# One-core transformer kernel: the feed-forward pipeline re-ordered and its residual added by TensorE, 71 expert tiles, an early square-root table, constants on GpSimd

## What is computed

```
x = x + 0.5 * ffn4(layernorm(x))     phase 0: FP4 feed-forward, hidden width 352
x = x + attn0(layernorm(x))          phase 1: low-rank causal attention
x = x + 0.5 * ffn4(layernorm(x))     phase 2
x = x + 0.5 * moe(layernorm(x))      phase 3: 8 experts, top 2, hidden width 512
x = x + attn1(layernorm(x))          phase 4: windowed attention
x = x + 0.5 * moe(layernorm(x))      phase 5

ffn4(x): g = q(x) @ q(w_gate).T;  u = q(x) @ q(w_up).T
         y = q(silu(g) * u) @ q(w_down).T
q(v):    per block of 16: scale = max|v| / 6, v / scale rounded to {0, .5, 1, 1.5, 2, 3, 4, 6}, times scale
moe(x):  each token goes to its 2 best experts:
         sum of weight * ((silu(x @ wg) * (x @ wu)) @ wd)
```

## Time and profile before

| what | value |
|---|---|
| median of three runs | 1475.54 us (1475.27 to 1479.11) |
| the profiled execution, its own time | 1479.2 us |
| its span, first to last instruction | 1477.4 us |
| mean granted TensorE clock | 0.895 |
| busy: TensorE, VectorE, ScalarE, GpSimd | 1116.1, 957.7, 823.1, 641.8 us |
| chain that ended last, by engine | TensorE 50%, VectorE 26%, DMA 6%, issue 6%, ScalarE 5% |

### The profile page before, as it was taken

One profiled execution on the slowest core, in us unless ns is written; L12 is line 12 of the kernel. 1 busy time (PEld: TensorE's weight loads), 2 busy tenths in 40 slices (PEclk: granted clock), 3 DMA queues, 4 the chain that ended last, 5 costly groups with the idle time before them and its releaser, 6 DMA issues.

```text
span 1477.4 us, 33914 instructions
## 1 busy us (share of the span) xinstructions
PE 1116.1 (76%) x11222; PEld 861.8 (58%) x11223; DVE 957.7 (65%) x1786; ACT 823.1 (56%) x1419; POOL 641.8 (43%) x924
## 2 busy tenths in 40 slices
PE   0577548999984776369999915998998636999991
PEld 0355425666653544259999902555554315999991
DVE  5799848888846997853333365889998385333333
ACT  0444236777654443246666662667766524666666
POOL 2122254344301222036766713666776302776671
PEclk9999959999997999669999956999999856999996
DMA  8100024333300000201111133353344020111115
GB/s 254 30 1 0 1 44 67 53 59 65 52 17 1 0 0 0 58 20 48 49 46 46 48 123 58 64 81 63 58 83 63 2 57 17 50 47 47 45 49 182
DMA packets 161060, 75.54 MB, mean 51 GB/s; under 512 B 125643, under 2 KB 153044, under 8 KB 160980
## 3 DMA queue, kind: packets, MB, share of 16 engines
q1 hardware_dynamic: 151508, 55.06, 17.6%
q0 software_dynamic: 9472, 19.42, 4.4%
HBM read 28.69 MB, written 15.86 MB: 30 GB/s over the span
## 4 chain that ended last, share of the span: by engine, by line
PE 50%; DVE 26%; DMA 6%; issue 6%; ACT 5%; SPq 4%; POOL 2%; DVEq 1%; ACTq 0%; POOLq 0%
PE PS L988 18%; PE PS L1008 9%; DVE m L772 4%; SPq L874 4%; PE PS L646 4%; PE PS L358 3%; PE PS L612 2%; PE PS L574 2%; DMA qT<-qs 2%; PE PS L628 2%; DVE q_amax L266 2%; DVE sg L772 2%; PE PS L654 1%; DVE q_xn L274 1%; PE PS L667 1%
## 5 line engine op out<-in xcount | busy, mean ns | idle before, releaser
L988 PE MATMUL PS<-xTs,pt 128*128 128x128 f32 x2336 | 287.5, 277 | 0.0
L988 PEld LDWEIGHTS PS<-xTs,pt 128*128 128x128 f32 x2336 | 275.7, 194 | 0.0
L1114 DVE TENSOR_TENSOR pt<-pt,PS 128x512 f32<-128x512 f32 x146 | 100.5, 688 | 237.4 <-PE PS L988 237.4
L720 ACT ACTIVATE pt<-PS 128x768 f32<-128x768 f32 (+1 forms) x256 | 225.8, 915 | 49.5 <-PE PS L574 24.5
L1233 POOL DMA_INDIRECT xs<-rows,src x152 | 147.2, 969 | 175.6 <-DVE src L1108 129.9
L1040 ACT ACTIVATE pt<-wgu 128x1024 f32 x148 | 156.3, 1057 | 89.4 <-issue 80.9
L1242 POOL DMA_INDIRECT outs<-ys,dst x144 | 142.0, 986 | 85.3 <-DVE ys L1122 78.2
L772 DVE TENSOR_REDUCE m<-PS 128x4 f32<-128x1024 f32 x128 | 153.2, 1221 | 25.3 <-PE PS L574 22.3
L1008 PE MATMUL PS<-wdn,pt 128*128 x1152 | 152.2, 275 | 0.0
L772 DVE TENSOR_REDUCE sg<-PS 128x6 f32<-128x768 f32 x128 | 118.2, 954 | 35.3 <-PE PS L574 33.2
L1008 PEld LDWEIGHTS PS<-wdn,pt 128*128 128x128 f32 x1152 | 140.0, 192 | 0.0
(11 more groups left out here) (235 smaller groups left out, 2071.6 us busy)
## 6 DMA issues: line engine op xcount, KB each, us to landing
pt<-outs SPq DMA_DIRECT2D x16, 512.0 KB, 5.2
rows<-qT SPq DMA_DIRECT2D x12, 256.0 KB, 2.4
xs<-rows,src POOLq DMA_INDIRECT x152, 2.5
outs<-ys,dst POOLq DMA_INDIRECT x144, 2.3
wgu<-in_L_ffn_w_gate SPq DMA_DIRECT2D x1, 2048.0 KB
wgu<-in_L_ffn_w_up SPq DMA_DIRECT2D x1, 2048.0 KB
wdn<-in_L_ffn_w_down SPq DMA_DIRECT2D x8, 256.0 KB
out<-X SPq DMA_DIRECT2D x8, 256.0 KB, 4.5
```

Of the source, the lines that this page charges most:

```text
L720: s.activation(k.pt[:, a % 4, :, 0:w], k.PS[:, self.bank:self.bank + 2, 0:w], ACT.Exp, scale=self.scale).then_inc(self.s_p, 1)
L988: last = t.matmul(k.PS[:, 1 + 2 * p + w, c * P:(c + 1) * P], k.wst[:, 1 - p, w, c * P:(c + 1) * P], k.xTs[:, p, :], start=True, stop=True)
L1114: v.tensor_tensor(k.hs[:, p, :], k.sgs[:, p, :], k.PS[:, 2 + 2 * p, :], ALU.mult).then_inc(self.s_h, 1)
```

## The change

Five edits. The diff is cut to its core; loops that only get a bound for the last tile are left out.

1. Feed-forward: the hidden values of pair z-3 (not z-2) are quantised in step z, statistics come for pair z-5, six steps stand ahead of the loop. Gate has its own semaphore and comes ahead of up. VectorE takes the statistics right behind the block maxima, no longer waits between these two, drops the instruction of line 273 (its constant goes into the division), and multiplies silu(gate) by up between the division and the rounding. X is added by TensorE as two more matmuls with the identity (four passes) behind the down product, w_down having been halved at the start, and ScalarE copies the sum to X.
2. NS = 71 expert tiles, NL = 71 columns of lists; nothing runs beyond the last tile; TensorE's loop has two passes of 24 tiles with 23 tiles written out behind it.
3. ScalarE takes the square root of one number ahead of its wait for the variances, in phases 1 to 5.
4. GpSimd makes `iotab` and the bias parts in phase 0 behind step 1, waiting for the weights; VectorE's part goes away.
5. `split_bias` waits behind each instruction.

In the diff the new parts of `Ffn` stand in the order VectorE, TensorE, ScalarE.

```diff
-NS = 72
+NS = 71
-NL = NS + RING
+NL = NS
...
     def scalar(self, eng, phase):
         k = self.k
+        if phase:
+            k.nc.scalar.activation(k.one[:, :], k.gone[:, :], ACT.Sqrt)
         eng.wait_ge(self.var, phase + 1)
...
-    STEPS, FIRST = N + 5, 4
+    STEPS, FIRST = N + 5, 6
...
+            v.scalar_tensor_tensor(xn.rearrange("p (n k) -> p n k", k=BLK), blocks, -NUDGE,
+                                   inv.unsqueeze(2).broadcast_to([P, n, BLK]), ALU.mult,
+                                   ALU.mult).then_inc(self.s_xn_read, 1)
 
         def fn(z, p):
+            if self.group(z):
+                largest(z, p)
+            if self.has(z - 5):
+                eng.wait_ge(self.s_added, x0 + z - 4)
+                for j in range(2):
+                    bn_stats(k, 2 * (z - 5) + j)
+            if self.group(z):
+                scaled(z, p)
+            if self.has(z - 2):
+                eng.wait_ge(self.s_up_ps, x0 + z - 1)
+                eng.wait_ge(self.s_silu, x0 + z - 1)
+                v.tensor_tensor(k.fxh[1 - p][:, HID:k.FW].rearrange("p (a b) -> p a b", a=2), k.sg[:, :, :],
+                                k.PS[:, 2:4, 0:I0], ALU.mult).then_inc(self.s_h, 1)
+            if self.group(z):
                 eng.wait_ge(self.s_sq, q0 + z + 1)
...
+            if x:
+                eng.wait_ge(self.s_xqT, x0 + z + 1)
+                if self.later(z):
+                    eng.wait_ge(self.s_silu, x0 + z)
+                for j in range(2):
+                    last = t.matmul(k.PS[:, j, 0:I0], k.xqT[:, j * P:(j + 1) * P], k.wguT[:, 0, :], start=True, stop=True)
+                last.then_inc(self.s_gate_ps, 1)
+                if self.later(z):
+                    eng.wait_ge(self.s_h, x0 + z)
+                for j in range(2):
+                    last = t.matmul(k.PS[:, 2 + j, 0:I0], k.xqT[:, j * P:(j + 1) * P], k.wguT[:, 1, :], start=True, stop=True)
+                last.then_inc(self.s_up_ps, 1)
+            if h:
+                eng.wait_ge(self.s_hqT, x0 + z - 2)
+                if self.later(z - 3):
+                    eng.wait_ge(self.s_added, x0 + z - 3)
+                for j in range(2):
+                    y = k.PS[:, 7, j * D:(j + 1) * D]
+                    for c, (o, w) in enumerate(HC):
+                        t.matmul(y, k.hqT[0:w, j, c, :], k.wdT[0:w, c, :], start=c == 0, stop=False)
+                    last = t.matmul(y, k.ident[:, :], k.X[:, ds(2 * (z - 3) + j, 1), :].squeeze(1), start=False, stop=True)
+                last.then_inc(self.s_y_ps, 1)
...
+            if self.has(z - 3):
+                eng.wait_ge(self.s_y_ps, x0 + z - 2)
+                s.activation(k.X[:, ds(2 * (z - 3), 2), :], k.PS[:, 7, 0:256].rearrange("p (a b) -> p a b", a=2),
+                             ACT.Copy).then_inc(self.s_added, 1)
...
-            gather(i + RING)
+            if i + RING < NS:
+                gather(i + RING)
...
+            def constants():
+                pool.wait_ge(s_w2, 16 * NW_LOADS)
+                ch.run(nc.gpsimd.tensor_copy(k.iotab[:, :], k.lists[:, 0:P]))
+                split_bias(nc.gpsimd, ch, k).then_inc(s_bias, 1)
+                pool.wait_ge(s_bias, 1)
+            kinds[0].constants = constants
...
-                if i == 1:
-                    dve.wait_ge(s_w2, 16 * NW_LOADS)
-                    ch.did(nc.vector.tensor_copy(k.iotab[:, :], k.lists[:, 0:P]))
-                    split_bias(nc.vector, ch, k).then_inc(s_bias, 1)
```

More of the change, by code:

```diff
@@ L209, in __init__ @@
         self.x0 = run * self.N
-        self.q0 = run * (self.N + 2)
+        self.q0 = run * (self.N + 3)
+        self.constants = None
         self.s_xn = k.sem("ffn_xn")
@@ L381, in normalised, with squared @@
             ins.then_inc(self.s_xn, 1)
+        def squared(z, p):
+            if self.group(z):
+                c = self.cols(z)
+                eng.wait_ge(self.s_xn_read, q0 + z + 1)
+                if self.has(z) and self.later(z, 2):
+                    eng.wait_ge(self.s_xq, x0 + z - 1)
+                if self.has(z - 5):
+                    eng.wait_ge(self.s_hq, x0 + z - 4)
+                s.activation(k.fmg[p][:, c], k.fxn[p][:, c], ACT.Square, scale=BINADE ** 0.5).then_inc(self.s_sq, 1)
         eng.wait_ge(self.k.sem("statistics_ready"), self.phase + 1)
@@ L919, in __init__ @@
         self.s_scaled = k.sem(name + "_scaled")
-        self.ld0, self.st0 = run * 16 * (NS // RING + 1), run * 16 * (NS // RING)
+        self.turns = [len(range(u, NS, RING)) for u in range(RING)]
+        self.t0 = [run * 16 * n for n in self.turns]
         self.ga0 = run * 16 * (NG // RING)
@@ L996, in tensor, with has, tiles @@
         up(0, 0, 1)
-        with eng.Fori(0, NS // UN) as m:
+        def has(n):
+            return not isinstance(n, int) or n < NS
+        def tiles(m):
             e = expert(UN * m)
@@ L1011, in tensor @@
                 e = e1
+        with eng.Fori(0, NS // UN) as m:
+            tiles(m)
+        tiles(NS // UN)
     def scalar(self, eng):
@@ L1058, in scalar, with has, tiles @@
         silu(0, 0)
-        with eng.Fori(0, NS // RING) as m:
+        def has(n):
+            return not isinstance(n, int) or n < NS
+        def tiles(m):
             for u in range(RING):
                 i, p = RING * m + u, u % 2
-                weights(i + 2, p, True)
-                silu(i + 1, 1 - p)
-                xT(i + 2, p, True)
+                if has(i + 2):
+                    weights(i + 2, p, True)
+                if has(i + 1):
+                    silu(i + 1, 1 - p)
+                if has(i + 2):
+                    xT(i + 2, p, True)
+        with eng.Fori(0, NS // RING) as m:
+            tiles(m)
+        tiles(NS // RING)
         for g in range(NG):
```

166 lines of the change are left out of this document (69 added, 97 removed).

## The result

The kernel after takes 1452.88 us in the median of four runs (1450.38 to 1454.82), the kernel before, run beside it, 1477.32 (1475.27 to 1480.39). The ratio is 0.9834, with a 95% interval of 0.9814 to 0.9854: 24.4 us less. The forecast was 1438, the range 1430 to 1455. So sign and range hold, and a third of the forecast gain is missing. Of the 15 us between 1438 and 1452.88, some 2 come from the kernel before, whose median here is 1477.32 and not the 1475.54 that the forecast started from.

What follows compares the result with a forecast made beforehand. VectorE was taken to bound feed-forward, TensorE the expert tiles. Terms 21.8 - 3 + 2.4 + 5.5 + 9.2 + 1.3 = 37.2 us off 1479.2 gave 1442.0 profiled, 1438 as median; range 1430 to 1455.

Steps and rivals of the forecast that it cites:

- A step on VectorE: Full feed-forward step: VectorE alone would need about 6.85 us instead of 7.69; as the bound, chance 0.12, time 1434.
- the new ring: Full feed-forward step: division, product, up, down with X, ScalarE's copy, statistics, next division at 7.03; sets steps of about 7.05 us.
- Number of steps: Each feed-forward phase: three input-only steps, 13 full, three with hidden values alone; gain 10.9 us per phase, 21.8 in two.
- hidden-only steps: End of each feed-forward phase: three steps with hidden values alone, 6.4 us each, ending at 161.0 instead of 172.5.
- the second full step at 6.4: Start of the full feed-forward steps: the first two steps have no statistics and take 6.4 us in all forecasts of length.
- the clock allowance: Feed-forward: one stretch of TensorE at its lower clock allowed in both phases, costing 3 us.
- TensorE's clock: Feed-forward: low stretches cost about 3 us each, one allowed; rival of six stretches, time 1455, chance 0.22.
- Constants: Phase 0: 4.7 us leave VectorE; about 7.5 us on GpSimd, priced at 2.3, between 0 and 5; net gain 2.4.
- Square-root table: Statistics of five phases: table load ahead of the wait gains 0.9 to 1.3 us each, 5.5 in all.
- The 13: Table loads: by the Trainium skill's drain of about 1.38 us, gain up to 2.66 each, 13 in all; not adopted.
- Experts: Expert phases: one tile fewer saves 2.79 us, last down product 1.85 sooner; 4.6 a phase, 9.2 in all.
- the lists: Expert lists, 568 elements instead of 608: about 0.04 us off two products per group, eight groups, two phases; 1.3 in all.

Runs made afterwards that it cites:

- b_scale: Kernel after with the reciprocal taken straight from the maxima and GpSimd's scale written behind the product, no guard for all-zero blocks: 1440.87 us, ratio 0.9744 to before.
- the fillers: Kernel after with three unused gate products (six passes) in each hidden-values-only step of the feed-forward, ahead of down: 1451.37 us, ratio 0.9819 to before.
- c_const: Kernel after with GpSimd's constants moved from behind step 1 to the end of phase 0: 1450.25 us, ratio 0.9814 to before.
- ab: Kernel after with statistics one step later, reciprocal straight from the maxima and GpSimd's scale behind the product, no all-zero guard: 1418.27 us, ratio 0.9597 to before.
- up_first: Kernel after with up's four passes put ahead of gate's again: 1522.1 us, ratio 1.0306 to before.

## Why the forecast was right in sign and 15 us too fast

**A step on VectorE and the new ring.** The ring is real and outside the loop about as long as forecast: b_scale's steps there are 6.65 to 6.76, and the scale of 0.2 that b_scale takes out makes it 6.9, against 7.03. Two things failed. In the loop the hand-over of ScalarE's copy to the statistics takes 0.26 us, where it is 0.03 outside, which makes it 7.3; the trace doesn't say why. And the step *"VectorE alone would need ... about 6.85 us"* summed VectorE's instructions at their lengths of before, though one of them depends on what GpSimd does at that moment. In before the scale began just when GpSimd's pieces had ended, at 145.58. GpSimd and VectorE, timelines of before:

```profile
143.61 1.97 POOL L312 TENSOR_TENSOR xhq<-qT,fscale 128x256 f32<-128x256 f32 x2 [5.82 <-DVE qT L288]
```
```profile
145.62 0.20 DVE L271 TENSOR_SCALAR fscale<-q_amax 128x60 f32<-128x60 f32 x1
```

The product of 0.88 us had stood ahead of the maxima and covered the pieces, unseen. I moved just this product away. The Trainium skill, "SBUF — State Buffer", section "Who interferes with whom", says that VectorE and GpSimd share a pair of ports as an exclusive lock, held for the whole instruction, for VectorE's two-port modes and for its instructions with two inputs in SBUF beside a GpSimd instruction that reads there. The rows agree: the scale ends with GpSimd each time (137.19 and 137.14, 144.46 and 144.40), and the rounding of 256 columns, which has two inputs in SBUF, took 1.24 beside the constants. The maxima, with one input, are 1.15 long either way. That the scale runs in a two-port mode no row shows; what the rows show is that it ends with GpSimd. Cost of both: the forecast had eleven steps 0.28 too short, 3.1 per phase, and the second full step at 6.4, which took 7.27: 0.9.

**Number of steps and the end of a phase.** The hidden-only steps were right (6.14 and 6.51 for 6.4). The tail was not: from 149.55 to the next phase's 178.96 are 29.4, where the forecast has 19.2 for three steps, 0.6, and before's 6.2 from 172.5 to the barrier: 26.0. I let the end of before's phase stand. But TensorE there has the down products of one more pair, and behind waits of 3.06 and 2.65 the clock is at the low level (0.63 from 165 us). With the fillers the same stretch is 26.75 (149.16 to 175.91), so the low clock is 2.7 of the 3.4. For phase 0 the account closes: 0.6 for a later first full step, 0.8 for the constants' step, 0.9, 3.1 and 3.4, less the 1.5 of the clock allowance that wasn't used, are 7.3 us, and the table lacks 7.2.

**TensorE's clock.** One low stretch among the full steps behind the opening was allowed, and one is there (the step from 466.11 to 475.05). It cost 8.94 - 7.35 = 1.6, not 3: gate and up took 2.55 and 2.43, but gate's extra runs before the product is ready. TensorE in after's phase 2, timeline; it answers to the earlier trace rows:

```profile
462.36 2.55 PE L371 MATMUL PS<-wguT,xqT 128*128 128x352 f32 x4
464.71 2.43 PE L376 MATMUL PS<-wguT,xqT 128*128 128x352 f32 x4
```

Where I erred was in looking at the full steps alone: the falls moved to the tails. From 68 to 143 us the granted clock is 1.00 in after although the transposes fill part of every step. So the rule of the Trainium skill, "TensorE: Matmul & The Clock Gate", section on the PE-mode transpose, which I had weighed, cost no full step there.

**Constants.** Length 7.98 for 7.5, removed from VectorE 4.76 for 4.7. The price was 3.8 (c_const), where I took 2.3 between 0 and 5; the lateness of Square was right, the roundings held beside GpSimd were missing. Net 1.0 for 2.4.

**Square-root table.** Right. ScalarE and VectorE in after's phase 1, timelines; they answer to the earlier trace rows:

```profile
179.00 1.28 ACT L181 ACT_TABLE_LOAD   x1
...
180.40 0.21 ACT L183 ACTIVATE std<-veps 128x32 f32<-128x32 f32 x1
```
```profile
180.64 0.35 DVE L170 RECIPROCAL rstd<-std 128x32 f32<-128x32 f32 x1 [0.39 <-ACT std L183]
```

The wait is 0.29 to 0.39 for 1.63 and more; the six statistics gained 6.7 for the 5.5 forecast. The 13 that follow from the drain which the Trainium skill names in "ScalarE: Activation LUTs", section on what a table load costs, are not there: the next instruction starts at 180.29, 0.01 after the load's end.

**Experts.** A tile is 2.79, the lists give 0.66 us a phase by the group's pitch (2.54 to 2.455, eight groups), as forecast. The last down product starts 1.64 behind the one before, where 2.79 is the rhythm: 1.15 us sooner instead of 1.85. In the phases' lengths only 0.75 of it is left (4.2 a phase, less 2.79 and 0.66); where the rest goes wasn't traced. TensorE at the end of after's phase 3, timeline; it answers to the earlier trace rows:

```profile
835.06 1.06 PE L1039 MATMUL PS<-wdn,pt 128*128 x8
836.70 1.15 PE L1039 MATMUL PS<-wdn,pt 128*128 x8 [0.58 <-DVE ys L1173]
```

No other product stands ahead of the last down product any more, but its single PSUM bank isn't free: the down product before it ends at 836.12, VectorE copies that result out from 836.16 to 836.45, and only then does the last one start. Its inputs were ready at 836.01. I had asked when the inputs are ready and when TensorE is free, not when the output is. No run tests this by itself.

**The sum.** Against the forecast in the profiled executions: feed-forward phases -15.6, tables +1.2, experts -2.1, and phases 1 and 4 +5.3, which nothing in the change explains. Together -11.2, and 37.2 - 11.2 is the 26 by which the spans differ. The last term was luck: in the profiles of the eleven other kernels phase 1 lasted 250.6 to 257.2 us and phase 4 289.2 to 294.0, with nothing in them changed, so before's 256.1 and 293.8 lie high. Without it after's profiled time would have been near 1458, above the range. Why these phases scatter wasn't tried and stays open.

## What to carry to other kernels

When work is moved off a bound engine, list every ring through the step and what the moved piece had been covering: two rings of 7.3 us left 0.5 us a step of the 1.25 that ab got (7.80 to 6.55), and taking one away gains 0 to 0.4 a step until the other goes too. The length of a VectorE instruction beside GpSimd is not its own. Read the tail of a phase by itself, with its clock, and for a last tile ask also when its output bank comes free.

## What the hardware showed that I had not expected

- A VectorE scale of 60 columns, 0.19 us alone, took 0.99 beside GpSimd's product (62.82 in after, with GpSimd from 61.80 to 63.76).
- With a TensorE wait of 3.3 us in each step the clock fell in nearly every step: 1.2 us more between product and down became 2.9 us a step, and the kernel took 44 us more than was priced for the ring alone (up_first).
- Six passes of products nobody uses, in a wait of 2.65 us, brought the down product from 1.65 back to 0.93 us.
